# Top-1 MoE of a fused two-layer kernel on one Trainium2 core: every token through all four experts, or tokens sorted by indirect transfers into 7 tiles, each with one expert

## Chip, cores and metric

One core of one Trainium2 chip runs the whole kernel. The metric is device microseconds (us) for one launch; the figure given is the median of several runs. PE is TensorE, DVE VectorE, ACT ScalarE, POOL GpSimd, SP the queue on SyncE that issues most DMAs.

## The reference, cut to what matters

Inputs are 16 batches of 512 tokens with 128 channels. Layer 0 adds to x a grouped-query attention (called A here) and a block with causal latent attention (M) and a mixture of experts; layer 1 adds a multi-query attention (B) and a gated FFN. All of it is float32. The part that the change touches:

```python
def moe(x, gate_w, gate_b, W1, b1, W2, b2):
    logits = x @ gate_w.T + gate_b
    top = jnp.argmax(logits, axis=-1)
    onehot = jax.nn.one_hot(top, N_EXPERTS, dtype=x.dtype)
    h = jax.nn.relu(jnp.einsum('btd,ehd->bteh', x, W1) + b1)
    y = jnp.einsum('bteh,edh->bted', h, W2) + b2
    return jnp.einsum('bted,bte->btd', y, onehot)
x = x + mla_attention(rmsnorm(x, norm1_w), ...)
x = x + moe(rmsnorm(x, norm2_w), gate_w, gate_b, W1, b1, W2, b2)
```

There are 4 experts with 512 hidden channels; each token needs one of them.

## The kernel before

**Tiles.** A batch is 4 tiles of 128 tokens. All weights, those of the 4 experts too (`w1s`, `w2s`), are loaded into SBUF once. Matmuls go through `in_columns` (line 522), which cuts the stationary operand into pieces of 32 columns, each in its own column group of the array; four such pieces stand side by side. One float32 matmul of the program is two MATMUL instructions in the trace, a bfloat16 one is one.

**Stages of a batch.** For each attention and each group of 4 heads there are `score_max` (scores on PE, row maximum on DVE, line 844, or with the causal mask line 849), `shift_split` and `shift_turn` (the maxima go into the queries by two small DMAs on SP, line 478), `score_exp` (scores again, exponential on ACT line 1045; for M also a mask on POOL, line 1192) and `probs_v`. Queries and keys are split in three bfloat16 parts on POOL and packed by 9 DMAs each on SP (`pack`, line 496).

**The MoE before.** `gate` computes logits and the winner's one-hot vector `oneh` (DVE lines 903 to 908, POOL lines 1217 to 1223). `up(e, c)` is 16 steps per batch: 128 hidden channels of one expert for all 512 tokens, bias and ReLU on DVE (line 922) for even steps and on ACT (line 1071) for odd ones. `down(e, half)` is 8 steps: 2 tiles of tokens times 4 chunks of 128 channels, and DVE adds the result times the one-hot column to `acc` (line 935). `add_b2` adds the chosen bias on POOL (lines 1231, 1232).

**What sets the order.** `stages()` (line 117) gives every step a time on a scale on which one batch takes 12 units (`PERIOD`); `ordered()` folds that scale, so that in the steady state one pass over 12 units works on three batches at once. Every engine walks the same table in its own instruction order and waits on semaphores; only the order counts, not the times. Here positions are counted as the table has them, with the `LEAD` of 1: `score_max` of M takes units 16 to 20, of A 20 to 24 and of B 24 to 28, which is 12 to 16 of the next pass; `score_exp` follows 1.99 units behind. The MoE's matmuls stand from 15.56 to 20.0. Seven PSUM banks (`BANKS`) are shared in rotation by all steps except `probs_v`, which has an eighth.

```python
BANKS, NPV = 7, 1
for s_last, value in last_user(b, turn_bank, m, name, k):
    pe.wait_ge(s_last, value)
```

Of the kernel before, what the change touches and what calls it, by code (L numbers as in the profile page):

```python
# [79 lines left out]
_at = 0  # L80
for _n, _w in (("a_bv", 32), ("a_bo", 128), ("gate_b", EXPERTS), ("b2", EXPERTS * D), ("b_bv", HD), ("b_bo", 128)):
    RCOLS[_n] = (_at, _at + _w)
    _at += _w
# [28 lines left out]
    "POOL": dict(x_norm=0.106, x1_norm=0.184, x2_norm=0.042, m_lat=0.1, gate=0.1, m_q=0.023, m_k=0.05, add_b2=0.0,  # L112
# [4 lines left out]
def stages():  # L117
# [80 lines left out]
def spare_users(name, *args):  # L198
# [22 lines left out]
def kernel_program(nc, x, w_all, w_lat, v_all, r_all, w1, w2, wi_up, wi_down, rope, out):  # L221
# [7 lines left out]
    with ctx:  # L229
# [14 lines left out]
        w1s = sb("w1s", [P, EXPERTS * HIDDEN])  # L244
        w2s = sb("w2s", [P, EXPERTS, HCH, D])
# [1069 lines left out]
```

## Time and profile before

| | us |
|---|---|
| runs | 2979.12, 2981.47, 2971.29; median 2979.12 |
| the profiled execution, own time | 2984.29 |
| its span (first to last instruction) | 2982.5 |
| mean granted TensorE clock in it | 0.98 |
| one steady pass of 12 units, from one x2 (line 876) to the next, 1349.9 to 1527.4 | 177.5 |

A busy share is the time in which an engine had at least one instruction under way. PE's instructions overlap, and their ends are modelled, so the distance from start to start is the better measure of what a matmul costs. The page's row of idle time names the instruction whose end let the engine go on.

### The profile page before, as it was taken

To read this page: it belongs to the slowest core of one execution; us is meant where nothing else is said; L and a number is where in the kernel's file an instruction comes from. 1 tells how busy PE (TensorE), PEld (TensorE's weight loads), DVE (VectorE), ACT (ScalarE), POOL (GpSimd) and SP (SyncE) were. 2 spreads that over 40 slices of the span, in tenths; PEclk is the share of its full clock that TensorE was granted. 3 is DMA by queue.
4 is the path that set the end of the run, shared out by engine and by line. 5 is a ranking of instruction groups with operands and counts; after the bars stand their busy time and mean duration, and the time that the engine had idled before them with its cause. 6 is when DMAs were issued, how large, how long until landed. Compare 5 with 4: busy or idle time off the path is not lost.

```text
span 2982.5 us, 116966 instructions
## 1 busy us (share of the span) xinstructions
PE 2787.7 (93%) x49280; PEld 1459.4 (49%) x49280; DVE 2351.8 (79%) x5811; ACT 1748.6 (59%) x3425; POOL 1038.6 (35%) x2006
## 2 busy tenths in 40 slices
PE   4979999999999999999999999999999999999978
PEld 1345454645545455454645545454454545545442
DVE  4768788797887978889797887979788797887835
ACT  1725656566565665656566565666656566565734
POOL 4243432334343333432334342233433333343110
PEclk7999999999999999999999999999999999999987
DMA  3010101101010010101101010110101001010000
GB/s 115 6 54 23 54 23 31 34 24 54 24 46 19 23 58 24 55 23 32 34 23 54 27 50 12 38 44 23 54 24 39 26 23 57 25 54 19 8 23 5
DMA packets 117452, 103.30 MB, mean 35 GB/s; under 512 B 19990, under 2 KB 116160, under 8 KB 116672
## 3 DMA queue, kind: packets, MB, share of 16 engines
q1 hardware_dynamic: 116928, 95.83, 10.5%
q8 instruction: 389, 6.37, 0.9%
q14 instruction: 135, 1.11, 0.1%
HBM read 8.56 MB, written 4.19 MB: 4 GB/s over the span
## 4 chain that ended last, share of the span: by engine, by line
PE 73%; DVE 19%; issue 4%; ACT 3%; POOL 1%; SPq 0%; DMA 0%; ACTq 0%; DVEq 0%; POOLq 0%
PE bank L526 52%; PE pv L644 17%; DVE mx L844 9%; PE bank L532 2%; PE bank L654 1%; DVE hid L949 1%; DVE hid L955 1%; DVE xn L741 1%; ACT hid L1078 1%; DVE bn L726 1%; DVE bank L849 1%; DVE latn L741 1%; ACT probs L1045 1%; DVE factored L741 1%; DVE l1bn L726 0%
## 5 line engine op out<-in xcount | busy, mean ns | idle before, releaser
L1045 ACT ACTIVATE probs<-bank 128x512 f32<-128x512 f32 x2688 | 1479.3, 597 | 855.6 <-PE bank L526 849.3
L844 DVE TENSOR_REDUCE mx<-bank 128x1 f32<-128x512 f32 x2048 | 1282.2, 682 | 81.4 <-PE bank L526 71.4
L849 DVE CUSTOM_DVE_ANT_0 bank<-bank,mask 128x128 f32<-128x128 f32 (+3 forms) x1024 | 480.4, 515 | 97.8 <-PE bank L526 97.6
L1192 POOL TENSOR_SCALAR_AFFINE_SELECT probs<-probs 128x256 f32<-128x256 f32 (+1 forms) x640 | 230.1, 362 | 765.8 <-ACT probs L1045 759.1
L526 PE MATMUL bank<-kp_B,qp_B 72*32 72x512 bf16 x4096 | 440.0, 394 | 28.7 <-DVE mx L844 24.5
L526 PE MATMUL bank<-kp_A,qp_A 72*32 72x512 bf16 x4096 | 403.7, 382 | 40.9 <-DVE mx L844 31.7
L526 PE MATMUL bank<-qp_B,kp_B 74*32 74x512 bf16 x4096 | 430.2, 384 | 1.4 <-ACT probs L1045 1.0
L526 PE MATMUL bank<-qp_A,kp_A 74*32 74x512 bf16 x4096 | 408.1, 382 | 0.5 <-ACT probs L1045 0.5
L526 PE MATMUL bank<-kp_M,qp_M 72*32 72x128 bf16 (+3 forms) x4096 | 332.7, 307 | 21.2 <-issue 16.0
L644 PE MATMUL pv<-probs,vv_B 128*32 128x512 f32 x2048 | 281.8, 601 | 9.3 <-ACT probs L1045 9.0
L526 PE MATMUL bank<-r2T,w1s 128*32 128x512 f32 x2048 | 281.1, 597 | 4.0 <-DVE hid L922 2.0
L644 PE MATMUL pv<-probs,vv_A 128*32 128x512 f32 x2048 | 269.1, 596 | 3.0 <-ACT probs L1045 2.8
L526 PE MATMUL bank<-qp_M,kp_M 74*32 74x128 bf16 (+3 forms) x4096 | 267.7, 302 | 0.8 <-DVE mx L844 0.4
L526 PE MATMUL bank<-w2s,hid 128*32 128x128 f32 x8192 | 249.7, 273 | 0.0
L526 PEld LDWEIGHTS bank<-w2s,hid 128*32 128x32 f32 x8192 | 229.5, 110 | 14.4 <-issue 5.8
L526 PEld LDWEIGHTS bank<-kp_B,qp_B 72*32 72x32 bf16 x4096 | 130.6, 98 | 192.2 <-issue 82.3
L526 PEld LDWEIGHTS bank<-qp_B,kp_B 74*32 74x32 bf16 x4096 | 139.1, 97 | 170.9 <-issue 100.2
L526 PEld LDWEIGHTS bank<-kp_A,qp_A 72*32 72x32 bf16 x4096 | 115.8, 96 | 201.9 <-DVE mx L844 88.7
L935 DVE SCALAR_TENSOR_TENSOR acc<-bank,oneh,acc 128x128 f32<-128x128 f32 x256 | 78.1, 347 | 171.1 <-PE bank L526 171.1
L526 PEld LDWEIGHTS bank<-kp_M,qp_M 72*32 72x32 bf16 x4096 | 137.8, 97 | 143.4 <-issue 88.3
L1175 POOL TENSOR_SCALAR nms<-mx 128x16 bf16<-128x16 f32 x192 | 39.1, 204 | 463.6 <-DVE mx L844 358.7
L526 PEld LDWEIGHTS bank<-qp_A,kp_A 74*32 74x32 bf16 x4096 | 120.1, 96 | 163.3 <-DVE mx L844 48.9
(144 smaller groups left out, 3276.8 us busy)
## 6 DMA issues: line engine op xcount, KB each, us to landing
qp_M<-parts_q SPq DMA_DIRECT2D x144, 128.0 KB
kp_M<-parts_k SPq DMA_DIRECT2D x144, 128.0 KB
qp_A<-parts_q SPq DMA_DIRECT2D x144, 128.0 KB
qp_B<-parts_q SPq DMA_DIRECT2D x144, 128.0 KB
kp_A<-parts_k SPq DMA_DIRECT2D x144, 32.0 KB
xs<-x SPq DMA_DIRECT2D x16, 256.0 KB, 3.1
out<-res SPq DMA_DIRECT2D x16, 256.0 KB, 2.2
kp_B<-parts_k SPq DMA_DIRECT2D x144, 8.0 KB
```

Source lines behind the costliest of these rows:

```text
L526: ins = pe.matmul(dst[at:at + n], lhsT[:, at:at + n], rhs, start=start, stop=stop, tile_position=(0, at))
L532: ins = pe.transpose(dst[:, P * t:P * t + P], src[:, t, :], ident[:])
L644: ins = pe.matmul(pv[0][32 * hh:32 * hh + VW, SEQ - q:SEQ], vv[a][:, c, VHEAD[a](GROUP * g + hh), :], probs[:, SLOT[a, g, u], col:col + q] ...
L654: ins = pe.transpose(m[:, P * t:P * t + P], osb[:, g % 2, P * t:P * t + P], ident[:])
L726: ins = v.bn_stats(bns[:, t, :], src[:, t, :])
L741: ins = v.tensor_scalar(dst[:, t, :], src[:, t, :], mvs[:, t, 0:1], rstd[:, t:t + 1], ALU.subtract, ALU.mult)
L844: v.tensor_reduce(mx[:, g % 2, at:at + 1], s1[BANK[a, g, u]][:], AX.X, ALU.max) \
L849: v.tensor_tensor_reduce(bank[:, 0:keys], bank[:, 0:keys], mask[:, SEQ - keys:SEQ], 1.0, LOWEST, ALU.add, ALU.max, mx[:, g % 2, at:at + 1] ...
L935: ins = v.scalar_tensor_tensor(out=acc[:, t, :], in0=m[:, P * j:P * j + P], scalar=oneh[:, t, e:e + 1], in1=acc[:, t, :], op0=ALU.mult, op ...
L1045: act.activation(probs[:, slot, :], s2[BANK2[a, g, u]][:], ACT.Exp).then_inc(sig[f"{a}_exp"], 1)
L1175: chain(b, f"{a}_nms", 2 * g + 1, pool.tensor_scalar(first, top, 1.0, 0.0, ALU.mult, ALU.add))
L1192: pool.affine_select(out=v, in_=v, compare_op=ALU.is_ge, fill=0.0, base=0, pattern=pattern, channel_multiplier=-1).then_inc(sig["M_masked" ...
```

## The change

The routing replaces computing all experts. After the one-hot vector: `ranks` (PE, matmuls with a triangle and with ones) counts, for each token, the tokens of the same expert before it; 12 small steps `route` on DVE turn this into a row number for each token and an expert number for each of 7 tiles (7 tiles of 128 rows always hold 512 tokens when each expert starts on a new tile). `scatter` (POOL, 4 indirect DMAs) writes the normed tokens to these rows of a DRAM buffer; `xp_in` (SP) reads all 7 tiles back; `xp_turn` transposes them. `weights` (SP) reads the expert's number from SBUF into a register and loads that expert's W1, b1, W2, b2 (128 x 1156 float32, 578 KB) into one of 3 slots, once for each of the 7 tiles. `up(j)` and `down(j)` are 7 steps each, on 128 tokens. `y_out` (SP, 2 DMAs) writes the results to DRAM, `gather` (POOL, 4 indirect DMAs) fetches them in token order, `moe_added` adds them to `acc`. The expert weights are no longer kept in SBUF, `add_b2` is gone, and the table's times for the MoE and what follows are new. At the start SP also fills the DRAM buffer with zeros. Core of the diff (in the order of the engines SP, PE, DVE, ACT, POOL):

```diff
+MOE_TILES = TILES + EXPERTS - 1
+MOE_ROWS = MOE_TILES * P
+WSLOTS, HSLOTS = 3, 3
...
-         x2_norm=0.352, e0=14.564, x2_scaled=-0.769, turn_r2=-0.5, gate=-0.174, step=0.2, down=0.03,
-         b0=0.311, x1_scaled=0.121, res1=0.75, turn_x1=0.513, b_q=0.8, split_bq=0.1, b_k=1.0, split_bk=0.228, b_v=1.19,
-         ff=1.0, ff_down=0.505)
+         x2_norm=0.352, e0=13.6, x2_scaled=-0.691, turn_r2=-0.5, gate=-0.318, ranks=0.157, route=0.15, route_step=0.044, scatter=0.75, xp_in=1.658, xp_turn=2.505, weights=0.724, up=2.9, step=0.246, later=0.3,
+         y_out=0.25, gather=0.618, moe_added=1.439, down=0.03,
+         b0=0.12, x1_scaled=0.121, res1=0.75, turn_x1=0.513, b_q=0.8, split_bq=0.1, b_k=1.0, split_bk=0.228, b_v=1.19,
+         ff=1, ff_down=0.505)
 
...
-    t = e0
-    for e in range(EXPERTS):
-        put(e0 + 0.15 * e, "add_b2", e)
-        for c in range(HCH):
-            put(t, "up", e, c)
-            t += step
-            if e and c in (1, 3):
-                put(t - step * 0.5, "down", e - 1, c // 2)
-                t += step
+    put(e0 + T["ranks"], "ranks")
+    for k in range(ROUTE):
+        put(e0 + T["route"] + T["route_step"] * k, "route", k)
+    for t in range(TILES):
+        put(e0 + T["scatter"] + 0.07 * t, "scatter", t)
+    put(e0 + T["xp_in"], "xp_in")
     for half in range(2):
-        put(t + T["down"] * (1 + half), "down", EXPERTS - 1, half)
+        put(e0 + T["xp_turn"] + 0.1 * half, "xp_turn", half)
+    for j in range(MOE_TILES):
+        t = e0 + T["up"] + step * j
+        put(t, "up", j)
+        put(t + T["later"], "down", j)
+        if j < WSLOTS:
+            put(e0 + T["weights"] + 0.02 * j, "weights", j)
+        if j + WSLOTS < MOE_TILES:
+            put(t + T["later"] + 0.2, "weights", j + WSLOTS)
+    t += T["later"]
+    for half in range(2):
+        put(t + T["y_out"] - (1 - half) * 3 * step, "y_out", half)
+    for half in range(TILES):
+        put(t + T["gather"] + 0.07 * half, "gather", half)
+    put(t + T["moe_added"], "moe_added")
+    t += T["moe_added"]
 
     b0 = t + T["b0"]
     put(b0, "x1_norm")
...
+            def xp_in(b):
+                sp.wait_ge(sig["r2_out"], total(b, "r2_out"))
+                if not b.first:
+                    sp.wait_ge(sig["y_out"], total(b.prev, "y_out"))
+                sp.dma_start(xp[:], rows(xq)).then_inc(sig["xp_loaded"], 16)
+
+            def weights(b, j):
+                slot = j % WSLOTS
+                sp.wait_ge(sig["route"], total(b, "route", TILE_EXPERTS))
+                for s_last, value in last_user(b, turn_weights, slot, "ys", j + 1):
+                    sp.wait_ge(s_last, value)
+                e = sp.value_load(tile_expert_i[0:1, j:j + 1], min_val=0, max_val=EXPERTS - 1)
+                sp.dma_start(wxs[:, slot, :], wx[bass.ds(e, 1)].rearrange("a p n -> p (a n)")) \
+                    .then_inc(sig[f"weights_{slot}"], 16)
+
+            def y_out(b, half):
+                first, end = ((0, TILES), (TILES, MOE_TILES))[half]
+                sp.wait_ge(sig["ys"], total(b, "ys", end))
+                if not b.first:
+                    sp.wait_ge(sig["moe_in"], total(b.prev, "moe_in"))
+                sp.dma_start(rows(yq)[:, first:end, :], xp[:, first:end, :]).then_inc(sig["y_out"], 16)
...
-            def up(b, e, c):
-                n = HCH * e + c
...
+                v.wait_ge(sig["up_ps"], total(b, "up_ps", j + 1))
+                for s_last, value in last:
+                    v.wait_ge(s_last, value)
+                m = misc[SPARE["hid_dve", j // 2 + 1]]
+                for c in range(HCH):
+                    ins = v.tensor_scalar(hid[:, j % HSLOTS, c, :], m[:, P * c:P * c + P], expert(j, "b1")[:, c:c + 1],
+                                          0.0, ALU.add, ALU.max)
+                ins.then_inc(sig["hid_dve"], 1)
+
+            def down(b, j):
+                v.wait_ge(sig["down_ps"], total(b, "down_ps", j + 1))
+                v.tensor_tensor(xp[:, j, :], misc[SPARE["ys", j + 1]][:, 0:D], expert(j, "b2"), ALU.add) \
+                    .then_inc(sig["ys"], 1)
+
+            def moe_added(b):
+                v.wait_ge(sig["moe_in"], total(b, "moe_in"))
+                v.wait_ge(sig["gqa_added"], total(b, "gqa_added"))
+                v.tensor_tensor(acc[:], acc[:], moe[:], ALU.add).then_inc(sig["acc_dve"], 1)
 
...
+            def xp_turn(b, half):
+                act.wait_ge(sig["xpT_ps"], total(b, "xpT_ps", half + 1))
+                if not b.first:
+                    act.wait_ge(sig["up_ps"], total(b.prev, "up_ps"))
+                first, end = ((0, SEQ), (SEQ, MOE_ROWS))[half]
+                act.activation(xpT[:, first:end], misc[SPARE["xpT_ready", half + 1]][:, 0:end - first], ACT.Identity,
+                               scale=vcol("norm2")).then_inc(sig["xpT_ready"], 1)
+
+            def up(b, j):
+                last = last_user(b, turn_hid, j % HSLOTS, "down_ps", j + 1)
+                if j % 2 == 0:
                     return
...
+                act.wait_ge(sig["up_ps"], total(b, "up_ps", j + 1))
+                for s_last, value in last:
+                    act.wait_ge(s_last, value)
+                m = misc[SPARE["hid_act", j // 2 + 1]]
+                for c in range(HCH):
+                    ins = act.activation(hid[:, j % HSLOTS, c, :], m[:, P * c:P * c + P], ACT.Relu,
+                                         bias=expert(j, "b1")[:, c:c + 1])
+                ins.then_inc(sig["hid_act"], 1)
...
-            def add_b2(b, n):
-
-                if n == 0:
-                    pool.wait_ge(sig["gqa_added"], total(b, "gqa_added"))
-                picked = four(rest[:])
-                b2 = rowv("b2")[:, D * n:D * n + D].unsqueeze(1).broadcast_to([P, TILES, D])
-                chain(b, "b2_term", n + 1, pool.tensor_tensor(picked, b2, spread(oneh[:, :, n], D), ALU.mult))
-                chain(b, "acc_base", n + 2, pool.tensor_tensor(acc[:], acc[:], picked, ALU.add))
+            def scatter(b, t):
+
+                if t == 0:
+                    pool.wait_ge(sig["route"], total(b, "route", ROWS_OF))
+                    if b.first:
+                        pool.wait_ge(ld_zero, 16 * 2)
+                    else:
+                        pool.wait_ge(sig["xp_loaded"], total(b.prev, "xp_loaded"))
+                pool.indirect_dma_start(xq, bass.IndirectOffsetOnAxis(ap=row_at_i[:, t:t + 1], axis=0),
+                                        factored[:, t, :], None).then_inc(sig["r2_out"], 16)
+
+            def gather(b, t):
+
+                if t == 0:
+                    pool.wait_ge(sig["y_out"], total(b, "y_out"))
+                    if not b.first:
+                        pool.wait_ge(sig["acc_dve"], total(b.prev, "acc_dve"))
+                pool.indirect_dma_start(moe[:, t, :], None, yq,
+                                        bass.IndirectOffsetOnAxis(ap=row_at_i[:, t:t + 1], axis=0)) \
+                    .then_inc(sig["moe_in"], 16)
...
```

Steps 3 to 6 and 8 to 10 of `route`, left out above, are one comparison, product, sum or addition each over at most 128 x 16 numbers. The walks of the engines take in the new steps, and the descriptor scratch of the program is set to 4096.

## Rows read from the trace of the kernel before

**Rows 1.** The page: busy shares and the last chain by engine.
```profile
PE 2787.7 (93%) x49280; PEld 1459.4 (49%) x49280; DVE 2351.8 (79%) x5811; ACT 1748.6 (59%) x3425; POOL 1038.6 (35%) x2006
...
PE 73%; DVE 19%; issue 4%; ACT 3%; POOL 1%; SPq 0%; DMA 0%; ACTq 0%; DVEq 0%; POOLq 0%
```

**Rows 2.** Windows, units 15 to 19; after the length PE, PEld, DVE, ACT, POOL busy.
```profile
1407.80:1424.60 16.80, 16.80 (x254) 7.91 (x256) 13.39 (x26) 11.47 (x23) 10.83 (x18) 1.00 0.27 81
1424.60:1440.40 15.80, 15.33 (x297) 9.05 (x290) 10.71 (x41) 10.51 (x21) 9.11 (x13) 1.00 0.27 84
1440.40:1455.40 15.00, 14.63 (x309) 9.28 (x305) 9.82 (x38) 9.41 (x19) 0.00 (x0) 1.00 0.03 7
1455.40:1470.40 15.00, 15.00 (x317) 8.91 (x321) 10.81 (x42) 7.89 (x16) 4.01 (x12) 1.00 0.05 15
1470.40:1484.40 14.00, 14.00 (x388) 10.75 (x381) 9.99 (x38) 6.25 (x12) 3.96 (x12) 1.00 0.04 11
```

**Rows 3.** Timeline of the last batch: start, length, engine, line, instructions merged.
```profile
2821.37 0.44 PE L526 MATMUL bank<-w,r2T 128*32 128x4 f32 x31
...
2829.46 1.04 PE L526 MATMUL bank<-r2T,w1s 128*32 128x512 f32 x8
...
2830.32 0.62 PE L526 MATMUL bank<-qp_B,kp_B 74*32 74x512 bf16 x8
...
2839.38 1.97 PE L526 MATMUL bank<-w2s,hid 128*32 128x128 f32 x64
...
2841.13 0.87 PE L526 MATMUL bank<-qp_B,kp_B 74*32 74x512 bf16 x12
```

**Rows 4.** The same windows for `w1s` alone: length, PE and PEld busy.
```profile
1424.60:1440.40 15.80, 4.48 (x32) 1.05 (x29) 1.00 0.27 84
...
1470.40:1484.40 14.00, 2.12 (x16) 0.58 (x16) 1.00 0.04 11
```

**Rows 5.** The same windows for `w2s` alone.
```profile
1424.60:1440.40 15.80, 1.96 (x64) 1.85 (x64) 1.00 0.27 84
...
1470.40:1484.40 14.00, 6.29 (x219) 5.77 (x212) 1.00 0.04 11
```

**Rows 6.** Groups by line and shape: count, busy us, mean ns, idle before.
```profile
L922 DVE TENSOR_SCALAR hid<-bank,vec 128x512 f32<-128x512 f32 x128 | 95.9, 749 | 53.4 <-PE bank L526 49.8
...
L1071 ACT ACTIVATE hid<-bank,vec 128x512 f32<-128x512 f32 x128 | 88.0, 688 | 113.1 <-PE bank L526 105.5 <-issue 7.6
L1232 POOL TENSOR_TENSOR acc<-acc,rest 128x512 f32<-128x512 f32 x64 | 81.7, 1277 | 5.0
L935 DVE SCALAR_TENSOR_TENSOR acc<-bank,oneh,acc 128x128 f32<-128x128 f32 x256 | 78.1, 347 | 171.1 <-PE bank L526 171.1
...
L532 PE MATMUL bank<-ident,factored 128*128 128x128 f32 x192 | 32.8, 296 | 26.4 <-ACT factored L1001 20.8 <-DVE factored L741 5.6
...
L1001 ACT ACTIVATE factored<-x,sq 128x128 f32<-128x128 f32 x64 | 20.3, 391 | 0.0
...
L903 DVE TENSOR_TENSOR lg<-bank,row 128x16 f32<-128x16 f32 x16 | 2.8, 175 | 5.4 <-PE bank L526 5.4
```

**Rows 7.** DMA issues by tile: KB each, median us from issue to landing.
```profile
xs<-x SPq DMA_DIRECT2D x16, 256.0 KB, 3.1
out<-res SPq DMA_DIRECT2D x16, 256.0 KB, 2.2
...
w1s<-w SPq DMA_DIRECT2D x1, 1024.0 KB, 4.8
```

**Rows 8.** Timeline of SP's queue, 1404 to 1424.
```profile
1408.72 3.21 SPq L496 DMA_DIRECT2D kp_M<-parts_k  x5
1414.71 1.20 SPq L478 DMA_DIRECT2D qp_B<-nmT  x2
```

**Rows 9.** Timeline of POOL and DVE, 1378 to 1381.
```profile
1378.71 1.28 POOL L1141 TENSOR_TENSOR res<-xs,row 128x512 f32<-128x512 f32 x1
1378.77 2.07 DVE L741 TENSOR_SCALAR xn<-xs,mv,sq 128x128 f32<-128x128 f32 x4
```

More of the change, by code:

```diff
@@ L50 @@
 HCH = HIDDEN // P
+MOE_TILES = TILES + EXPERTS - 1
+MOE_ROWS = MOE_TILES * P
+WSLOTS, HSLOTS = 3, 3
+XCOLS = {}
+_at = 0
+for _n, _w in (("w1", HIDDEN), ("b1", HCH), ("w2", HCH * D), ("b2", D)):
+    XCOLS[_n] = (_at, _at + _w)
+    _at += _w
+XN = _at
+CCOLS = {}
+_at = 0
+for _n, _w in (("before", P), ("ones", P), ("counts", EXPERTS * TILES), ("below", EXPERTS * EXPERTS),
+               ("places", MOE_TILES * (EXPERTS - 1))):
+    CCOLS[_n] = (_at, _at + _w)
+    _at += _w
+CN = _at
+ROUTE = 12
+TILE_EXPERTS, ROWS_OF = 8, 12
 FF1 = 384
@@ L218, with kernel_program @@
 LAST = 2
[L221 removed]
+def kernel_program(nc, x, w_all, w_lat, v_all, r_all, consts, wx, xq, yq, wi_up, wi_down, rope, out):
     table = ordered()
@@ L243, in kernel_program @@
         row = sb("row", [P, RN])
-        w1s = sb("w1s", [P, EXPERTS * HIDDEN])
-        w2s = sb("w2s", [P, EXPERTS, HCH, D])
+        cst = sb("cst", [P, CN])
+        wxs = sb("wxs", [P, WSLOTS, XN])
         wgu = sb("wgu", [P, 2 * FF1])
@@ L334, in kernel_program @@
             declare(name, per)
+        for slot in range(WSLOTS):
+            declare(f"weights_{slot}", 16 * len(range(slot, MOE_TILES, WSLOTS)))
         for s in ("mq", "mk", "aq", "ak", "bq", "bk"):
@@ L501, in o_proj @@
                     sp.dma_start(batch(out, b), res1[:]).then_inc(sig["y_stored"], 16)
-            walk({"x_load": x_load, "shift_turn": shift_turn, "pack": pack, "o_proj": o_proj},
+            walk({"x_load": x_load, "shift_turn": shift_turn, "pack": pack, "o_proj": o_proj,
+                  "xp_in": xp_in, "weights": weights, "y_out": y_out},
                  ordered(LATE["SP"]))
@@ L674, in gate, with ranks @@
                 ins.then_inc(sig["gate_ps"], 1)
[L676 to L691 removed]
+            def ranks(b):
+                if b.first:
+                    pe.wait_ge(ld_const, 16)
+                m = misc_bank(b, "route", 1)
+                pe.wait_ge(sig["one_hot"], total(b, "one_hot"))
+                chosen = oneh[:].rearrange("p t e -> p (t e)")
+                n = TILES * EXPERTS
+                in_columns(m[:, 0:n], const("before"), chosen, True, False)
+                for t in range(1, TILES):
+                    in_columns(m[:, EXPERTS * t:n], const("ones"), chosen[:, 0:n - EXPERTS * t], False, t == TILES - 1)
+                for t in range(TILES):
+                    ins = in_columns(m[:, n:n + EXPERTS], const("ones"), chosen[:, EXPERTS * t:EXPERTS * t + EXPERTS],
+                                     t == 0, t == TILES - 1)
+                ins.then_inc(sig["ranks_ps"], 1)
@@ L972, in _ @@
                          score_max=score_max, out_turn=out_turn, o_proj=o_proj,
-                         x2_norm=x2_norm, gate=gate, up=up, down=down,
+                         x2_norm=x2_norm, gate=gate, route=route, up=up, down=down, moe_added=moe_added,
                          x1_norm=x1_norm, ff_up=ff_up, ff_down=ff_down)
```

218 lines of the change are left out of this document (137 added, 81 removed).

## The prediction

> **What bounds the kernel now.** I read the page's shares first: PE is busy 93% of the span, DVE 79%, and the chain that ended last runs over PE for 73% [rows 1]. PE's ends are modelled, so the share alone proves little; the windows cut at the starts of units 15 to 19, where the MoE stands, say more. In those 76.6 us PE is busy 75.8, DVE 54.7 and ACT 45.5 [rows 2]. So where the MoE is computed PE is the bound, and DVE has 22 us of room. That matters because outside these units DVE is close behind PE, and what PE loses there would buy less. The granted clock is 1.00 in all five windows, that is 2.4 GHz.
>
> All in all the case is PE time saved in a stretch that PE bounds, against a long new chain through POOL, SP and DRAM.
>
> **What the change takes from PE, for one batch.** Start to start, 8 instructions on `w1s` take 0.86 us (0.1075 each), 64 on `w2s` take 1.75 (0.0273 each), 31 of the gate's small ones at most 0.44 (0.0142 each) [rows 3]. Removed: `up` 16 x 4 x 2 = 128 instructions, 13.8 us; `down` 8 x 2 x 4 x 4 x 2 = 512 instructions, 14.0 us; together 27.8. Added: 7 tiles x 4 chunks x 4 pieces x 2 = 224 instructions for `up` and as many for `down`, all with 128 moving columns like those on `w2s`: 448 x 0.0273 = 12.2 us. Seven transposes at 32.8/192 = 0.17 [rows 6]: 1.2. `ranks` has 8 calls of `in_columns`, 64 instructions of at most 16 columns; the nearest row is the gate's: 0.9. Net: 27.8 - 14.3 = 13.5 us less.
>
> A rule against the small matmuls: the gate's 31 need at most 14.2 ns each, while the Trainium skill, TensorE: Matmul & The Clock Gate, section "Wait — 56ns, not 53.3ns?", says that start to start never drops below about 25 ns. By that rule `ranks` would be 1.6 us instead of 0.9 and the whole sum 11 us longer; the trace does not agree, at least for pieces of 32 columns side by side, and I go by the row.
>
> **What comes of it stretch by stretch.** A unit cannot get shorter than its next engine. Unit 16 (1424.6 to 1440.4) loses 32 + 64 instructions [rows 4, 5], 3.4 + 1.7 = 5.2 us, and would fall from 15.8 to 10.6; ACT there has 10.5 with about 1.3 of hidden activations that move away (5.5 us of line 1071 over 4.4 units), 9.2 left, so I take 11.2. Unit 19 (1470.4 to 1484.4) loses 16 + 219, 7.7 us, and keeps two `down` (1.7): 8.0, with DVE at 10.0 - 2.5 + 0.6 = 8.1 there [rows 2, 6]; two engines with equal work don't overlap fully, so I take 8.2. Together 0.8 us are not cashed in, and 12.7 us for one batch remain. Over the 16 batches that is 203 us.
>
> **DVE, ACT, POOL.** DVE loses the work of lines 922 and 935, (95.9 + 78.1)/16 = 10.9 us, and gains 16 quarter activations and 7 bias additions at line 935's 78.1/256 = 0.31 (7.0), 12 routing steps at 0.18 (2.1) and one whole addition (at most 0.75): 9.9. ACT trades the 88.0/16 = 5.5 us of line 1071 for 12 x 0.32 and two copies of xp at up to 0.69, 5.2 [rows 6]. Both changes are near zero and hidden beside PE; if PE were no longer the bound, they would still be no loss. POOL loses more than 4 x 1.28 = 5.1 us in line 1232 alone [rows 6] and gains 8 indirect DMAs.
>
> **The price of an indirect DMA on POOL.** The trace has none. Call the time that one holds POOL c. Below, no less than SP needs to issue a pack, 3.21/5 = 0.64 us [rows 8]; above, POOL might be held until its data land, 1.28 for its largest present operation plus 3.1 for a 256 KB read [rows 6, 7]: 4.4. I take 1.3, POOL's largest row, since making 128 addresses is work on one short list, no transfer.
>
> **The new chain, part one.** Routing ends at position 15.24, the transposes stand at 17.10. In the new unit lengths (about 14.7, 11.2, 12.7 us) that is 0.76 x 14.7 + 11.2 + 1.3 = 24 us. Needed: 4c + 2.2 to land [rows 7] + 0.6 issue + 3.5 to read 448 KB (between the rows of 256 KB, 3.1, and 1024 KB, 4.8) = 11.5 us at c = 1.3, and 24 at c = 4.4. I cost it at nothing; its cover is the attention work of the two other batches, and at c above 4.4 PE would stand still. Only the first batch, which has less beside it, may pay some 10 us once.
>
> **SP and the weights.** SP gets, per batch, 7 register reads, 7 weight loads, `xp_in` and two `y_out`. The first three weight loads sit between the packs of `kp_M` and need `route` step 8; behind them wait the packs and B's shift. SP has 1414.71 - 1411.93 = 2.8 us of idle there [rows 8], and three reads with loads take at least 3 x 0.64 = 1.9; with the register reads 3 to 5. Also 1.7 MB go ahead of that small shift in the queue. PE and ACT then wait for the shift: 0 to 4 us, I take 1.5. The later loads need the slot of three tiles before: `weights(j + 3)` stands 0.238 units, 3.2 us, ahead of its `up`, and needs 0.6 + a register read + 3.8 (578 KB by the same two rows), about 5 us. PE is late by 1.8 once; the following loads are spaced like their tiles and don't add. Bounds 0 to 4 us.
>
> **The new chain, part two.** `gather` stands at 19.89, where POOL also masks M's probabilities (10 a unit), and `probs_v` stands 0.21 units, about 3 us, behind its exponentials. POOL held for 4c makes the masks late: 4c - 3 = 2.2 us at c = 1.3. After the gather, `moe_added` has 0.82 units (about 11 us) for 4c + 2.2 = 7.4: hidden. What is queued behind it on DVE is the score maxima of A, and all of PE's banks wait for these.
>
> **The sum.** Stalls 1.5 + 1.8 + 2.2 = 5.5 us less 0.5 that I let overlap: 5.0. Gain 12.7 - 5.0 = 7.7 us for a batch, 123 us for 16. The profiled execution took 2984.3, 5.2 above the median of the runs shown; 2984.3 - 123 = 2861, on the median's scale 2856 us.
>
> **The rivals.**
> (a) Nothing stalls: the slack in positions and the banks absorb all three waits. For it: SP is idle most of the time, and PE and ACT have queues. Against it: B's shift already comes after a wait of SP. 2979 - 203 = 2776 us.
> (b) PE is no longer the bound and the rest eats the gain: units 16 and 17 are then paced by ACT and DVE with semaphore round trips between three nearly equal engines, and the weight waits come at each tile (7 x 1.8 = 12.6 us) because SP's register read and the load are longer than the tiles' spacing. 12.7 - 12.6 is nothing: about 2977, range 2930 to 2988. Against it: the loads of different slots overlap.
> (c) Slower: POOL. If one indirect DMA holds POOL for 4.4 us, the gather blocks the masks for 17.6 us, PE waits 14.6 of them in `probs_v`, and with the other stalls (1.5 + 1.8) a batch loses 17.9 against 12.7: 16 x 5.2 = 83 us, 3062 us. It decides from c = 3.1 on, where 4c - 3 and these 3.3 reach 12.7. For it: POOL is slow at everything, and it shares something with DVE: four `xn` operations took 2.07 us, 0.52 each against 0.31 for line 935's of the same size, and POOL had begun one of 1.28 us just before them [rows 6, 9].
> The Trainium skill, SBUF — State Buffer, section "Who interferes with whom", has this as a lock that also keeps POOL from writing descriptors while DVE runs certain copies from SBUF to SBUF. Here the trace shows such a wait for DVE only; the DVE work beside scatter and gather reads mostly PSUM. If each of the 8 transfers were held by one operation of 0.31 us, that would be 2.5 us a batch, 40 us, still faster than before (2896).
>
> **How the numbers follow.** Forecast 0.60 (own range 2800 to 2925), (a) 0.12, (b) 0.12, (c) 0.12, the lock 0.04. A measurement of this kernel can tell about 0.3%, 9 us, from no change. Of (b) 0.05 lie within it and 0.03 above; so faster 0.60 + 0.12 + 0.04 + 0.04 = 0.80, same 0.05, slower 0.12 + 0.03 = 0.15. The range 2772 to 2965 takes in (a), the lock and the faster part of (b), and leaves out (c) and the rest of (b), 0.20.
>
> **What would show it.** PE instructions on the expert weights fall from 640 to 448 a batch and a pass from 177.5 to about 170 us; the windows of units 16 and 19 shorten most; DVE's share rises to about 83% with nearly the same busy time. POOL's indirect DMAs show c. Idle PE before `up` is the weight stall; idle PE before `probs_v` of M, ended by POOL's masks, the gather; idle PE before B's last exponentials, ended by a DMA, the shift. The forecast is wrong if c is beyond 3.1 us, if DVE rather than PE ends the waits in units 15 to 19, or if the first transposes wait for `xp_in` in every pass.

## The result and the profile after

The changed kernel takes 3013.4 us in the median of four runs (3011.62 to 3022.93), the kernel before 2979.3 beside it: 1.0126 times the time before, 95% interval 1.0097 to 1.0154. It is 1.3% slower where 4% less was forecast, and outside the range. The profiled execution took 3022.93 us.

The page of the changed kernel, its engines, the granted clock in 40 slices, its DMA queues and the last chain:

```profile
PE 2691.6 (89%) x47344; PEld 1435.9 (48%) x47344; DVE 2349.8 (78%) x6003; ACT 1736.0 (57%) x3521; POOL 1018.5 (34%) x2006
...
PEclk7979999999999999999899999999899999999987
...
DMA packets 168021, 190.82 MB, mean 63 GB/s; under 512 B 24614, under 2 KB 150736, under 8 KB 167504
...
HBM read 84.18 MB, written 16.25 MB: 33 GB/s over the span
...
PE 69%; DVE 13%; issue 7%; POOL 4%; DMA 3%; ACT 2%; SPq 1%; ACTq 0%; DVEq 0%; POOLq 0%
```

Against [rows 1] PE has 1936 instructions fewer (121 for each batch, as the count of the parts gives) and is busy 96 us less, and DVE's busy time is the same within 2 us. So the work did go. But PE's share fell from 93 to 89%, "issue" and DMA grew in the chain, and the mean granted clock is 0.932 where it was 0.98.

The time per pass shows where the saving went. I take the 11 passes from the third x2 to the fourteenth and charge every matmul with its start-to-start time at 2.4 GHz (512 columns 0.213 us, 128 columns 0.053, float32 twice that, four column groups side by side counted once). "Half clock" is what the same work took more at a granted clock of 0.5, and "idle" is the rest:

| mean of a pass, us | length | PE's work | idle | half clock |
|---|---|---|---|---|
| before | 178.2 | 162.4 | 15.0 | 0.8 |
| after | 180.6 | 149.1 | 22.6 | 8.9 |
| difference | +2.4 | -13.3 | +7.6 | +8.1 |

The work is the trace's instructions at these prices and not a measured duration. PE's work fell by 13.3 us, and 15.7 us of waiting and slow clock took its place. The largest hole is one that no pass had before. Timeline of the changed kernel, SP's queue and then PE, in pass 7, from the x2 of batch 7 at 1359.9 to the next (the brackets give the idle time before and what ended it):

```profile
1419.11 1.26 SPq L583 DMA_DIRECT2D kp_M<-parts_k  x2
1421.70 3.35 SPq L536 DMA_DIRECT2D wxs<-wx  x3
1425.10 2.09 SPq L583 DMA_DIRECT2D kp_M<-parts_k  x3
1427.23 1.28 SPq L565 DMA_DIRECT2D qp_B<-nmT  x2
1428.55 2.89 SPq L583 DMA_DIRECT2D kp_M<-parts_k  x4
1431.56 1.89 SPq L583 DMA_DIRECT2D qp_A<-parts_q  x3
1433.55 0.42 SPq L528 DMA_DIRECT2D xp<-xq  x1
...
1430.59 0.38 PE L614 MATMUL bank<-qp_B,kp_B 74*32 74x512 bf16 x1
1437.63 0.30 PE L614 MATMUL bank<-kp_M,qp_M 72*32 72x128 bf16 x4 [6.66 <-issue]
```

Between `kp_M`'s second and third pack stand three weight loads, 1.7 MB, and with the register reads they hold SP for 4.7 us, from the end of the second pack at 1420.4 to the third at 1425.1. The last pack is issued by 1431.44, the last landing of the packs is recorded at 1437.54, and M's first score starts at 1437.63, 6.2 us behind the issue. PE stands still for 6.66 us, and in 14 passes (the first two batches left out) for 4.5 to 9.7, 6.0 in the mean. Windows of the changed kernel over the same stretch (length; PE, PEld, DVE, ACT, POOL busy; granted clock, DMA share, GB/s):

```profile
1422.00:1426.00 4.00, 4.00 (x65) 1.94 (x61) 3.78 (x8) 2.97 (x8) 2.87 (x3) 1.00 0.79 224
1426.00:1430.00 4.00, 4.00 (x56) 1.76 (x52) 3.79 (x7) 2.59 (x5) 3.50 (x5) 1.00 0.92 332
1430.00:1434.00 4.00, 0.97 (x13) 0.27 (x5) 1.47 (x3) 1.09 (x2) 1.63 (x4) 0.99 0.54 180
1434.00:1438.00 4.00, 0.37 (x8) 0.29 (x12) 0.00 (x0) 0.00 (x0) 0.31 (x1) 0.50 0.80 199
1438.00:1442.00 4.00, 4.00 (x44) 1.63 (x40) 1.49 (x9) 1.94 (x4) 3.20 (x4) 0.50 0.55 152
1442.00:1448.00 6.00, 6.00 (x88) 2.82 (x84) 3.03 (x13) 2.75 (x6) 0.00 (x0) 0.54 0.11 36
```

The DMA engines are 79 and 92% busy while the packs should land. Then PE has next to nothing to do, and the granted clock goes to 0.50 (1.2 GHz) and stays there for 13.7 us, most of it after the work is back. In the same place the kernel before looks otherwise. Its windows, and below them its timeline, SP and then PE:

```profile
1416.00:1420.00 4.00, 4.00 (x59) 1.84 (x52) 3.17 (x6) 2.25 (x4) 3.75 (x4) 1.00 0.34 97
1420.00:1424.00 4.00, 4.00 (x59) 1.96 (x58) 3.13 (x5) 2.55 (x6) 3.67 (x5) 1.00 0.18 50
```

```profile
1415.95 2.69 SPq L496 DMA_DIRECT2D kp_M<-parts_k  x4
...
1415.19 1.07 PE L526 MATMUL bank<-r2T,w1s 128*32 128x512 f32 x8
1418.22 1.07 PE L526 MATMUL bank<-r2T,w1s 128*32 128x512 f32 x8
...
1422.38 1.02 PE L526 MATMUL bank<-r2T,w1s 128*32 128x512 f32 x5
1422.84 0.23 PE L526 MATMUL bank<-kp_M,qp_M 72*32 72x128 bf16 x3
```

There the last pack was issued by 1418.6, 4.2 us ahead of M's first score, and the first `up` products of the MoE, three of them at 0.86 us each, ran in the 8 us before that score. In the changed kernel the MoE's first product comes 20 us after M's first score, so this work, which covered a part of the landing, has gone from the place as well.

There is a second stretch at half clock in every pass, 7 to 14 us in all, that begins 59 to 71 us behind M's first score. PE waits there for POOL's `nms`, which stands behind the gather and M's masks, and the MoE's `down` products [rows 5] no longer run beside it. Timeline of the changed kernel, POOL and PE:

```profile
1491.99 1.01 POOL L1400 DMA_INDIRECT moe<-yq,row_at_i  x1 [0.31 <-issue]
1493.00 0.42 POOL L1350 TENSOR_SCALAR_AFFINE_SELECT probs<-probs 128x256 f32<-128x256 f32 x1
1493.59 0.96 POOL L1400 DMA_INDIRECT moe<-yq,row_at_i  x1 [0.16 <-issue]
...
1497.80 0.22 POOL L1334 TENSOR_TENSOR nms<-mx,nms 128x16 bf16<-128x16 f32 x1
...
1498.16 0.22 PE L703 MATMUL bank<-identb,nms 128*32 128x128 bf16 x1 [1.50 <-POOL nms L1334]
```

### The profile page after: what moved, and what is told of

It reads as the page before. It is cut to its first block, busy times and chain, and to the rows that moved or that the text cites. A ratio compares the mean times of both kernels' runs of the same rounds, so it can differ in the third digit from the quotient of the medians.

```text
span 3021.2 us, 114225 instructions
## 1 busy us (share of the span) xinstructions
PE 2691.6 (89%) x47344; PEld 1435.9 (48%) x47344; DVE 2349.8 (78%) x6003; ACT 1736.0 (57%) x3521; POOL 1018.5 (34%) x2006
## 4 chain that ended last, share of the span: by engine, by line
PE 69%; DVE 13%; issue 7%; POOL 4%; DMA 3%; ACT 2%; SPq 1%; ACTq 0%; DVEq 0%; POOLq 0%
PE bank L614 47%; PE pv L732 17%; DVE mx L959 7%; DMA wxs<-wx 2%; PE bank L620 2%; POOL moe L1400 2%; PE bank L742 2%; ACT probs L1197 1%; POOL probs L1350 1%; DVE xn L854 1%; DVE bank L964 1%; DVE bn L839 1%; SPq L583 1%; PE bank L784 1%; DVE factored L854 0%
## 5 line engine op out<-in xcount | busy, mean ns | idle before, releaser
L614 PE MATMUL bank<-kp_M,qp_M 72*32 72x128 bf16 (+3 forms) x4096 | 342.4, 322 | 116.1 <-issue 83.8
L614 PE MATMUL bank<-kp_A,qp_A 72*32 72x512 bf16 x4096 | 417.7, 407 | 24.8 <-DVE mx L959 22.4
L732 PE MATMUL pv<-probs,vv_B 128*32 128x512 f32 x2048 | 298.4, 638 | 5.0 <-ACT probs L1197 4.9
L614 PE MATMUL bank<-qp_M,kp_M 74*32 74x384 bf16 (+3 forms) x4096 | 286.8, 317 | 17.2 <-DVE mx L959 16.6
L614 PEld LDWEIGHTS bank<-kp_A,qp_A 72*32 72x32 bf16 x4096 | 124.8, 100 | 185.5 <-DVE mx L959 69.1
L732 PE MATMUL pv<-probs,vv_M 128*32 128x512 f32 (+3 forms) x2048 | 199.2, 473 | 11.3 <-POOL probs L1350 6.4
L614 PEld LDWEIGHTS bank<-qp_M,kp_M 74*32 74x32 bf16 x4096 | 140.0, 101 | 116.7 <-issue 41.1
L964 DVE DVE_READ_ACCUMULATOR2_ANT mx<- 128x1 f32 x1024 | 145.4, 142 | 0.0
L614 PE MATMUL bank<-xpT,wxs 128*32 128x128 f32 x3584 | 125.0, 276 | 15.7 <-DMA wxs<-wx 13.0
```

The source lines that it names most:

```text
L614: ins = pe.matmul(dst[at:at + n], lhsT[:, at:at + n], rhs, start=start, stop=stop, tile_position=(0, at))
L732: ins = pe.matmul(pv[0][32 * hh:32 * hh + VW, SEQ - q:SEQ], vv[a][:, c, VHEAD[a](GROUP * g + hh), :], probs[:, SLOT[a, g, u], col:col + q] ...
L964: v.tensor_tensor_reduce(bank[:, 0:keys], bank[:, 0:keys], mask[:, SEQ - keys:SEQ], 1.0, LOWEST, ALU.add, ALU.max, mx[:, g % 2, at:at + 1] ...
```

## The experiments

Each ratio is against the kernel before on the same chip; after itself is 1.0126 [1.0097, 1.0154]. "The hole" is PE's idle time ahead of M's first score.

**The loads behind the packs.** The table's time of the first three weight loads, nothing else.

```diff
-weights=0.724
+weights=1.16
```

> The changed kernel, with the first three weight loads (register read and transfer) moved in SP's order behind all nine packs of kp_M instead of behind the second. Theory Q (SP's queue: these three loads hold up the last seven packs, PE stands idle 7 us at the first causal score maximum of each batch, and the clock is then at 1.2 GHz for about 14 us, in which PE loses some 5 more): the hole falls under 2 us, that clock stretch goes, 10 to 12 us a batch are won, total 2820 to 2860 us. Rival R (the hole is the routing chain itself, or DMA traffic of scatter and xp that stays where it is): hole at least 5 us, total over 2980 us.

Measured: 3019.1 us, 1.0137 [1.0112, 1.0162]. The time lies above the first theory's range although the hole shrank as it says, to 1.1 us in pass 7: another of 8 us opened that ends 19 us further on. Timeline of this kernel, SP and PE:

```profile
1435.55 3.08 SPq L536 DMA_DIRECT2D wxs<-wx  x3
1438.75 2.44 SPq L583 DMA_DIRECT2D qp_A<-parts_q  x3
1441.30 0.43 SPq L528 DMA_DIRECT2D xp<-xq  x1
1441.77 6.20 SPq L583 DMA_DIRECT2D qp_A<-parts_q  x5
1448.01 1.21 SPq L565 DMA_DIRECT2D qp_B<-nmT  x2
...
1455.70 0.62 PE L614 MATMUL bank<-qp_B,kp_B 74*32 74x512 bf16 x4 [8.01 <-DMA qp_B<-nmT]
```

B's shift, two DMAs of 4 KB, was issued from 1448.0 on behind `xp_in` and eight packs of A, and the last of it landed 7.7 us later. The wait was moved, not removed: here the small transfer that was needed next paid.

**No register read.** The loads take a fixed expert number, so SP reads no register; the choice of the expert by the routing is left out.

```diff
-e = sp.value_load(tile_expert_i[0:1, j:j + 1], ...)
-sp.dma_start(wxs[:, slot, :], wx[bass.ds(e, 1)]...)
+sp.dma_start(wxs[:, slot, :], wx[j % EXPERTS])
```

> The changed kernel with fixed expert numbers (j modulo 4) for the weight loads: no register read on SP, same waits, same place in the order, same bytes. The choice of experts by routing is left out. Tells SP's own time from the transfers' traffic. If the hole comes from SP's time in the three reads (about 1.6 us a load in the profile against 0.35 for the issue alone), it shrinks by 3 to 4 us, total about 2940 us or less. If it comes from 1.7 MB of weights ahead of the packs in the DMA queues, it stays above 5 us and the total stays within 1% of 3013 us.

Measured: 2989.7 us, 1.0037 [1.0009, 1.0066]; the hole in pass 7 is 5.0 us. The reads cost 24 us, 1.5 a batch; most of the hole is not theirs.

**No weight traffic.** Register reads and instructions stay, the bytes go: later batches compute with the weights of the first.

```diff
+n = XN if b.first else 4
-sp.dma_start(wxs[:, slot, :], wx[bass.ds(e, 1)]...)
+sp.dma_start(wxs[:, slot, 0:n], wx[bass.ds(e, 1)]...[:, 0:n])
```

> The changed kernel with the register reads and issues of all weight loads in place, but after the first batch each moves only 4 columns (2 KB) instead of 1156 (578 KB): later batches compute with the weights of the first. If the traffic makes the hole, it falls under 2 us and the total to about 2850 us; if SP's time does, hole and total change little (over 2970 us).

Measured: 2942.8 us, 0.9891 [0.9874, 0.9909], 71 us less than the changed kernel: the bytes cost 4.4 us a batch. The hole in pass 7 is still 3.2 us and the half clock 7.6 us a pass, and the time lies between the two ranges, so the bytes are not all of it.

**Is PE time worth what the windows said?** The kernel before, less 12.1 us of PE's MoE work a batch.

```diff
+                if c < 2:
+                    in_columns(m[:], w1s[:, P * n:P * n + P], r2T[:]).then_inc(sig["up_ps"], 1)
+                else:
+                    in_columns(m[:], identb[:], identb[:].unsqueeze(1).broadcast_to([P, TILES, P])) \
+                        .then_inc(sig["up_ps"], 1)
...
-                    for c in range(HCH):
+                    for c in range(2):
```

> The kernel before, with part of its MoE left out on PE alone: half of the hidden chunks get cheap bfloat16 matmuls in place of their float32 ones, and down sums two chunks instead of four. PE loses 5.1 + 7.0 = 12.1 us a batch, nearly what the change saves (13.3), with nothing added and all DVE, ACT and POOL work as before. If PE time in this stretch is worth what the windows say, it gains 10 to 12 us a batch: 2790 to 2820 us, the clock stays at 0.98. If other engines or a falling clock take it back, over 2880 us.

Measured: 2819.5 us, 0.9469 [0.9449, 0.9489]: 158 us, 9.9 a batch, with no half clock beyond that of the kernel before. So PE does bound the stretch, and less work in place does not by itself bring the clock down.

**The loads alone, in the kernel before.** No register reads and no routing; all experts use the first one's `w1`, with the same work, to make room for the buffer.

```diff
+for j in range(7):
+    put(13.6 + 0.724 + 0.02 * j if j < 3 else 13.6 + 3.4 + 0.246 * (j - 3), "weights", j)
...
+sp.dma_start(spare_w[:, slot, :], w2...[:, 0:1156]).then_inc(sig[f"weights_{slot}"], 16)
```

> The kernel before with the weight loads alone: seven plain loads of 4.6 KB a row (4.1 MB a batch) by SP, at the places in the order that the changed kernel gives its own, into a buffer that nothing reads; to make room for it, all four experts use the first one's `w1`, with the same work. No routing, no register reads, TensorE's work as before. If the loads in front of M's packs are the cause, a hole of 3 to 6 us opens ahead of M's first score and the clock falls behind it: 3040 to 3130 us. If the kernel before has the slack for them that I gave the changed one (a stall of up to 1.5 us a batch): 2975 to 3005 us.

Measured: 3044.1 us, 1.0207 [1.0173, 1.0242], 63 us more than before: 3.9 a batch, the price that taking the bytes away gave from the other side. The time is in the range of the first theory, but the hole that it wanted, 3 to 6 us in each batch, is not there: where `up` products still ran it is 0.1 us in pass 7 and 1.0 in the mean of 14 passes (0 to 3.8), and the half clock 1.8 us a pass (0.8 before). With the same loads and no register reads in the changed kernel, the run above, it is 4.4 in the mean. The two kernels differ in more than the `up` products, in the routing's own transfers for one, but the loads alone don't make the hole.

**A's packs later.** The nine packs of A's queries 0.52 units and those of its keys 0.2 later, with the loads behind M's packs as in the first experiment.

```diff
-put(t + T["pack"] + 0.06 * r, "pack", s, r)
+put(t + T["pack"] + {"aq": 0.52, "ak": 0.2}.get(s, 0.0) + 0.06 * r, "pack", s, r)
```

> As e1 (first weight loads behind the packs of kp_M), and the packs of qp_A and kp_A, which are needed only 37 to 50 us later, moved 0.52 and 0.2 units back in SP's order, so that B's last shift (4 KB) and xp are issued before them. In e1 PE stood 8.0 us for that shift, landed 7.7 us after its issue behind packs, weights and xp. Theory Q2 (a small transfer waits in SP's order and behind the backlog of 16 DMA engines; whatever PE needs next is then late): with the backlog moved away both holes fall under 2 us and the first stretch at 1.2 GHz goes; 10 to 12 us a batch, total 2830 to 2870 us. Rival (the DMA engines simply have too much to carry in this stretch, whatever the order): a hole of 4 us or more stays, total over 2960 us.

Measured: 2910.2 us, 0.9778 [0.976, 0.9797]: 103 us less than the changed kernel, and faster than before, but above the first theory's range. Timeline of this kernel, SP and PE:

```profile
1384.72 2.68 SPq L583 DMA_DIRECT2D kp_M<-parts_k  x4
1389.25 3.11 SPq L536 DMA_DIRECT2D wxs<-wx  x3
1392.47 0.39 SPq L528 DMA_DIRECT2D xp<-xq  x1
1397.05 1.22 SPq L565 DMA_DIRECT2D qp_B<-nmT  x2
1398.38 6.00 SPq L583 DMA_DIRECT2D qp_A<-parts_q  x9
...
1390.49 0.24 PE L614 MATMUL bank<-kp_M,qp_M 72*32 72x128 bf16 x4 [0.88 <-issue]
```

Packs of M, loads, `xp_in`, shift, packs of A: nothing urgent stands right behind anything large, and 4.2 us lie between the end of `xp_in`'s issue and the shift. The hole is 0.9 us, the one ahead of B's shift is gone, and the first stretch at half clock has gone with them. The same edit of the packs without the move of the loads:

> The changed kernel with A's packs later and the weight loads where they were (one of the two edits of the 2910 us version). The loads then still go ahead of M's packs. If the hole ahead of M's first score maximum (6.7 us) is their doing, it stays at 5 to 7 us and the time at 2975 to 3015 us; if A's packs, which then no longer stand in front of the shift, were the crowd, it closes and the time is 2905 to 2930 us.

Measured: 3015.0 us, 1.0133 [1.0113, 1.0153], with the hole at 5.6 us in pass 7. Neither edit is worth anything alone.

**Does the idle time lower the clock?** In the changed kernel PE repeats a product of B 24 times where it waits for M's packs. The packs come no sooner.

```diff
+if a == "M" and n == 0:
...
+    for _ in range(0 if b.i - b.o < 2 else 24):
+        in_columns(s1[BANK[a, g, u]][:, :], q_rows("B", 0, ROWS1)[:, 0:P], k_rows("B", 0, ROWS1))
```

> The changed kernel, in which TensorE repeats one head's score product of layer B 24 times (some 5.1 us of work, at 0.21 us for four matmuls of 512 columns) where it waits for M's packs; the result is overwritten by M's first score. The packs come no sooner. If the clock falls to 1.2 GHz because TensorE stands idle there, it stays at 2.4 GHz through that stretch, the 13.7 us at half clock behind it go, and the kernel becomes faster by 3 to 6 us a batch although it does more: 2920 to 2970 us. If the clock falls for another reason (what the other engines or the transfers draw), it falls all the same, and the time is 3000 to 3040 us.

Timeline of this kernel, PE in pass 7, and its windows:

```profile
1428.05 5.53 PE L614 MATMUL bank<-kp_B,qp_B 72*32 72x512 bf16 x93
1433.86 0.24 PE L614 MATMUL bank<-kp_M,qp_M 72*32 72x128 bf16 x4 [0.28 <-DMA kp_M<-parts_k]
```

```profile
1430.00:1434.00 4.00, 3.73 (x70) 2.08 (x63) 0.00 (x0) 0.00 (x0) 0.13 (x1) 1.00 0.69 210
1434.00:1442.00 8.00, 7.66 (x161) 4.15 (x161) 5.68 (x27) 6.24 (x13) 3.40 (x4) 1.00 0.50 140
```

Measured: 2991.7 us (2972 to 3011 in nine runs, 3027 in a tenth), 1.0023 [0.9991, 1.0055], so about 20 us less than the changed kernel with 5.1 us of useless work more in each batch, and between the two ranges that I gave. In pass 7 the clock held at 1.00 with DVE and ACT standing still and DMA at 69%, where it had fallen to 0.50. In 14 passes the first stretch at half clock came in eight, for 3.4 to 10.2 us, instead of in all, for 6.8 to 13.7. The filling did not always reach: in the eight passes 1.6 to 4.9 us of the hole were left, in five of the other six 0.3 to 0.8, in the sixth 2.3. So PE's own idle time brings the clock down there. That is no way to run the kernel, but it prices the fall.

**The second stretch.** Two runs had seven more products ahead of A's first shift. That was the wrong place, 14 us behind the wait for `nms`, which is that of M's last shift.

> The 2910 us version (loads behind the packs, A's packs later), in which TensorE repeats a score product of layer M seven times (1.5 us of work) ahead of A's first shift, where it waits 1.5 us for POOL's `nms`. If the idle time there drops the clock, the second stretch at half clock goes and the time is 2860 to 2895 us. If the thin work after it drops the clock, or the other engines do, the time stays at 2905 to 2935 us.

Measured, on the 2910 us version: 2956.4 us, 0.9915 [0.9883, 0.9948]. In pass 7 the seven products ran at half clock and took 3 us, in front of scores that were due. The time is above both ranges. The run says nothing about that wait, but it gives a price for PE work on the path: 1.5 us a batch at full clock cost 46 us, 2.9 a batch.

> The changed kernel with both pieces of filling work (24 products ahead of M's packs, seven ahead of A's first shift), and nothing moved. If both falls of the clock come from TensorE's idle time, both stretches go, 6 to 10 us a batch: 2860 to 2925 us. If neither does: 3010 to 3060 us.

Measured: 3025.3 us, 1.0165 [1.0112, 1.0218]; the same misplacement on top of the filled first hole, so the time says nothing for either theory. In the right place, ahead of M's last shift:

```diff
+if a == "M" and g == 3 and b.i - b.o >= 2:
+    for _ in range(7):
+        in_columns(m[:, :], q_rows("M", 0, ROWS1)[:, 0:P], k_rows("M", 0, ROWS1))
```

> The 2910 us version with seven repeated products of layer M (1.5 us of work) ahead of M's last shift, which is where the wait of 1.5 us for `nms` stands (the two runs with filling work ahead of A's first shift had it 14 us too late, where nothing waits). If the idle time ahead of this shift is behind the second stretch at half clock, that stretch shrinks or goes, as the first did when its hole was filled: 2860 to 2900 us. If the stretch comes from the waits for DVE that stand 7 to 10 us later, it stays and the filling hides in the wait: 2905 to 2925 us.

Measured: 2905.8 us, 0.9739 [0.9723, 0.9755], level with the version without it, and the second theory's range. The work hides in the wait, the wait before `nms` is gone, and the second stretch still comes, in each of 14 passes, for 6.8 to 10.2 us. PE's timeline and windows of this kernel:

```profile
1451.16 0.40 PE L614 MATMUL bank<-qp_M,kp_M 74*32 74x512 bf16 x4 [1.16 <-DVE mx L962]
1453.81 1.04 PE L614 MATMUL bank<-kp_A,qp_A 72*32 72x512 bf16 x8 [1.38 <-DVE mx L962]
```

```profile
1443.00:1449.00 6.00, 6.00 (x125) 2.89 (x113) 5.61 (x10) 3.04 (x6) 3.69 (x11) 1.00 0.05 13
1449.00:1455.00 6.00, 3.35 (x48) 0.84 (x40) 5.68 (x19) 1.79 (x3) 2.50 (x7) 0.89 0.01 3
1455.00:1461.00 6.00, 6.00 (x57) 3.05 (x57) 3.91 (x7) 2.62 (x5) 2.29 (x4) 0.54 0.02 4
```

The fall follows two waits for DVE's score maxima with PE busy 3.35 of 6 us and DVE 5.68. The kernel before has such a pair too, of 1.10 and 0.90 us at 1490 and 1493. Its windows there:

```profile
1486.00:1492.00 6.00, 4.90 (x85) 2.30 (x81) 5.93 (x19) 3.59 (x8) 3.63 (x10) 1.00 0.02 5
1492.00:1498.00 6.00, 5.10 (x95) 2.36 (x90) 6.00 (x13) 3.42 (x6) 2.51 (x5) 1.00 0.01 3
```

DVE is as full, but PE has 4.90 and 5.10 us of work in 6, and the clock is 1.00. That this thin work is the cause fits, but filling these two waits wasn't tried, so what brings the clock down in the second stretch is argued and not shown.

**POOL and the gather.** Four plain reads by SP in the place of the four indirect ones (the rows come in the tiles' order, so which token gets which result is left out).

```diff
-pool.indirect_dma_start(moe[:, t, :], None, yq, ...)
+sp.dma_start(moe[:, t, :], rows(yq)[:, t, :])
```

> The changed kernel with the four indirect gathers on POOL replaced by four plain reads of yq on SP at the same places: the rows come back in sorted order, so which token gets which result is left out. POOL loses 4 x 0.95 us a batch while it masks M's probabilities. If POOL's hold makes the second loss (PE waited 1.7 us for POOL's nms and about 1 us for masks), 2 to 6 us a batch are won, total 2915 to 2980 us; if not, within 0.3% of 3013 us.

Measured: 2985.7 us, 1.0029 [1.0015, 1.0043], 28 us less, 1.7 a batch, between the two ranges. The same on the 2910 us version:

> The 2910 us version with four plain reads of the 128 rows in order by SP in the place of the four indirect ones (the rows come in the tiles' order, so the output is another). POOL is then free of 3.8 us a batch. In the changed kernel this was worth 28 us. If POOL's hold is behind the second stretch at half clock here too: 2850 to 2885 us; if that stretch comes from the thin work of TensorE whatever POOL does: 2895 to 2915 us.

Measured: 2890.1 us, 0.972 [0.9676, 0.9764], 20 us less, again between the ranges; its interval just touches that of the 2910 us version. With the bytes of the loads gone instead:

> The 2910 us version with the weight loads cut to 4 of 1156 columns after the first batch (the multiplications then use the first batch's weights: the output is another). If the order of the transfers already hides the 4 MB of weights a batch, 2900 to 2915 us; if the traffic still takes time from the packs and the shift: 2860 to 2890 us.

Measured: 2879.6 us, 0.9667 [0.9649, 0.9685]: good order leaves 31 of the 71 us that the bytes cost.

**Moving the gather.** With the real gather no other place was better. In the changed kernel 0.22 units earlier, and the same on the 2910 us version:

> The changed kernel with gather 0.22 units and moe_added 0.44 units earlier in the table, so that all of layer 1's projections move 0.44 units forward, near to where they stood before the change. For the second stretch at 1.2 GHz (138 to 155 us into a pass, some 5 to 6 us a batch): if PE lacks work there because the MoE's end comes late in the table, the clock stays high or falls later and 3 to 6 us a batch are won, total 2920 to 2965 us; the first hole stays. If it is gather on POOL holding the masks, nothing or a loss: 3000 us or more.

> e5 and e6 together. If the two holes are independent, the gains add: 13 to 17 us a batch, total 2750 to 2830 us, faster than the kernel before. If only one of them can be had, as e5 or e6 alone.

Measured: 3043.9 us, 1.0223 [1.0206, 1.024], and 2946.4 us, 0.9886 [0.9869, 0.9902]. The waits for `nms` go and waits of 1.2 and 2.2 us for M's masks come (pass 7 of the first). A smaller step on the 2910 us version (0.618 to 0.5):

> The 2910 us version with the four gathering transfers 1.7 us earlier and the addition of the MoE where it is. If POOL then has the last shift's `nms` out in time, the 1.5 us wait goes and with it 1 to 3 us a batch: 2865 to 2895 us. If they then push M's masks back by as much (as the version with the gather 3.2 us earlier showed), 2905 to 2950 us.

Measured: 2951.4 us, 0.99 [0.9885, 0.9915], with a wait of 2.4 us for the masks in pass 7. And later (0.8, the addition at 1.6):

> The version with the loads behind the packs and A's packs later (2910 us), and with the four gathering transfers 2.0 us and the addition of the MoE 1.8 us later, so that they stand behind the first shift of layer 1 on POOL. If the wait of 1.7 us for `nms` in front of the second stretch at half clock is what POOL's gather costs, it goes, and with it 3 to 8 us a batch: 2785 to 2860 us. If what matters is that the gather and the masks take turns at all, the wait only moves to the next shift or to DVE's addition: 2900 to 2930 us.

Measured: 3015.4 us, 1.0115 [1.0098, 1.0132], worse than either case I had named; pass 7 shows 2.1 us of waiting ahead of `probs_v` of M and 3.2 ahead of a score of A.

**The hole in all of these.** PE's idle time ahead of M's first score, us, from the traces:

| kernel | mean of 14 passes | lowest to highest | pass 7 |
|---|---|---|---|
| before | 0.0 | 0.0 to 0.0 | 0.0 |
| before, with the loads | 1.0 | 0.0 to 3.8 | 0.1 |
| changed | 6.0 | 4.5 to 9.7 | 6.7 |
| changed, no register read | 4.4 | 3.4 to 8.0 | 5.0 |
| changed, no bytes | 2.7 | 2.2 to 3.9 | 3.2 |
| changed, A's packs later | 5.7 | 4.9 to 7.7 | 5.6 |
| changed, loads behind M's packs | 1.0 | 0.8 to 1.4 | 1.1 |
| changed, both | 1.0 | 0.8 to 1.6 | 0.9 |

## Why the prediction was wrong

**PE's work: right.** 13.5 us less were forecast, and the trace's instructions at the table's prices give 13.3; the kernel with 12.1 us less work in place shows that such time is worth 9.9 a batch. So 2.2 were not cashed in there, where I had taken 0.8 for the change (the floors of units 16 and 19).

**DVE, ACT, `ranks`: right.** DVE's busy time changed by 2 us in 2350. `ranks` goes by the row, not by the page's rule. Timeline of the changed kernel:

```profile
1413.03 0.70 PE L614 MATMUL bank<-oneh,cst 128*32 128x16 f32 x62
```

62 instructions start within 0.7 us, 11 ns each. The Trainium skill, TensorE: Matmul & The Clock Gate, section "Wait — 56ns, not 53.3ns?", has 25 ns as the least distance; no trace here supports it for pieces side by side.

**The indirect DMA: c between the bounds, near the lower one.** It holds POOL for 0.96 us (median of the scatter's 64; 0.95 for the gather), taken at 1.3. The gather's stall was put at 2.2 us and is 1.7 by the run without it. It shows at M's last shift, not where I had put it, at `probs_v`. Rival (c) needed 3.1 and is out. So is the rival with the lock, which wanted 0.31 us more on each: the 64 gathers take 0.94 to 1.02 us, the 64 scatters 0.95 to 1.23.

**The chain through POOL, SP and DRAM: right at nothing.** The transposes of `xp` have 0.0 us of idle time ahead of them, although `xp_in` takes 7.1 us to land and not 3.5. Groups of the changed kernel:

```profile
L784 PE MATMUL bank<-ident,xp 128*128 128x128 f32 x112 | 20.1, 298 | 0.0
...
L614 PE MATMUL bank<-xpT,wxs 128*32 128x128 f32 x3584 | 125.0, 276 | 15.7 <-DMA wxs<-wx 13.0 <-issue 1.9 <-ACT probs L1197 0.5
```

**Weights at their tiles: sized too high.** 1.8 us a batch forecast, 13.0/16 = 0.8 measured, so rival (b)'s 7 x 1.8 didn't come.

**"SP and the weights": the step that failed.** SP's own time came as forecast: 4.7 us for three reads and loads, where the text has "3 to 5". It says that "1.7 MB go ahead of that small shift in the queue", bounds the wait by "0 to 4 us, I take 1.5", and names the shift as what suffers. The place was right, the sufferer and the size wrong. M's packs pay first, with a hole of 6.66 us in pass 7 and 4.5 us at the least in 14 passes, all above my upper bound. Bytes cost 4.4 us a batch and register reads 1.5 by the runs without each; if these two added, they would be 5.9. I had summed SP's issue time and had not asked what DMA engines at 79 to 92% do to the transfers behind.

**A cover that I did not count.** The prediction subtracted the MoE's products as if their place in the pass didn't matter. They stood in two thin places, while M's packs landed and beside DVE's maxima at the other end. Moved away, they leave PE idle there. At M's packs the two runs without register reads bear this out: 4.4 us of hole without the `up` products and 1.0 with them. No run puts such work back into the changed kernel as part of its own, so how much of the hole is the missing cover stays open; 2.6 us of `up` products had stood there. At the other end it is argued only.

**The clock: missing altogether.** I read 1.00 in all five windows and took it as given. In the sum it is 8.1 us a pass, as large as the added idle time. The hole ahead of M's packs costs twice: its length, and the work behind it at 1.2 GHz. None of the three signs that I named for a wrong forecast looks at the clock or at M's packs.

The sum then stands as follows. Forecast -12.7 + 5.0 = -7.7 a batch. Measured (passes) -13.3 + 7.6 + 8.1 = +2.4. The 5.0 us of stalls and the 0.8 not cashed in stand against 7.6 of idle time, not far off in sum though not in place; without the 8.1 of the clock the sum would have kept its sign (-5.7). The slower side was given 0.15, but by another mechanism. What can be had: the order of the transfers alone brings 2910 us, 2.2% faster than before, and 5.2 us a pass still go to the half clock.

## What to carry to other kernels

Before work is taken off the bounding engine, ask what each piece of it covers where it stands, a transfer in flight or a wait for another engine, because PE may then stand idle in that place. Bulk loads belong behind every small transfer that someone needs soon, and an order has to be found for all of them together: here each of two moves was worth nothing alone and both were worth 103 us. Read the granted clock as something that the change can alter, and price a new hole in PE with the slow work behind it.

## What the runs showed of the hardware

- The granted clock fell from 2.4 to 1.2 GHz within or just behind a stretch in which PE was nearly idle (0.97 and then 0.37 us busy of 4), and stayed low for 7 to 14 us, also after PE was full again. It held when PE was given useless work there. It also fell where PE was busy 3.35 of 6 us in short waits, but not in the kernel before at 4.9 of 6.
- Two DMAs of 4 KB had landed 7.7 us after the first of them was issued, behind about 1.7 MB of loads, 448 KB of `xp_in` and eight packs.
- Three register reads with their loads hold SP for 4.7 us, about 1.6 each (pass 7 of the changed kernel); without the reads the three loads take 1.4 (in the kernel before with loads).
- An indirect DMA of 128 rows of 512 B holds POOL for 0.95 to 0.96 us, on the scatter and on the gather; the gather's data land 2.4 to 3.7 us after issue.
